# Edge gates of a graph-network kernel: one float32 product from the loaded features in place of three products from a rounded lead and rest

## What is computed

```
x_norm = layernorm(h);  q, k, v = x_norm @ Wq.T + bq, x_norm @ Wk.T + bk, x_norm @ Wv.T + bv
dk = silu(edge_attr @ Wdk.T + bdk)          # the "gates": 64 -> 256
dv = silu(edge_attr @ Wdv.T + bdv)          # 64 -> 256
attn = sum(q[dst] * k[src] * dk, axis=1)    # one number for an edge
attn = silu(attn) * cosine_cutoff(r)
msg  = v[src] * dv * attn[:, None]
agg  = segment_sum(msg, dst);  out = x + agg @ Wo.T + bo
```

## Time and profile before

| | |
|---|---|
| Median of 3 runs | 3666.56 us (3665.77 to 3671.32) |
| The profiled execution | 3659.42 us |
| Its span, first to last instruction | 3657.6 us |
| TensorE's granted clock, mean | 0.974 |
| TensorE busy | 3381.2 us, 92% of the span |
| VectorE busy | 3185.6 us, 87% |
| ScalarE busy | 2594.7 us, 71% |
| GpSimd busy | 2390.0 us, 65% |

### The profile page before, as it was taken

The page is one execution under the profiler, slowest core; times in us unless marked ns, Lnnn a source line. Parts: engine busy times, 40 slices in busy tenths (PEclk is TensorE's granted clock), DMA queues, the critical chain, the costliest instruction groups (busy, mean ns, idle before and its releaser), DMA issues. The chain is left out here.

```text
span 3657.6 us, 111781 instructions
## 1 busy us (share of the span) xinstructions
PE 3381.2 (92%) x25829; PEld 2771.8 (76%) x25830; DVE 3185.6 (87%) x9898; ACT 2594.7 (71%) x7607; POOL 2390.0 (65%) x2549
## 2 busy tenths in 40 slices
PE   3979999999999997996999999999999999997997
PEld 2547777777777775775888888888888888886996
DVE  6768999999999995664999999999999999996775
ACT  1856777777777774543878888888888888884553
POOL 3756777777777763554666666666666666663775
PEclk8989999999999997998999999999999999998998
DMA  3979999999999984776888888888888888884663
GB/s 102 263 230 309 301 296 301 298 298 298 299 298 300 300 253 165 276 258 224 254 235 239 240 236 239 237 239 237 238 238 239 238 237 239 236 237 150 213 208 126
DMA packets 604966, 898.40 MB, mean 246 GB/s; under 512 B 208971, under 2 KB 418646, under 8 KB 604371
## 3 DMA queue, kind: packets, MB, share of 16 engines
q0 software_dynamic: 164240, 566.71, 50.5%
q1 hardware_dynamic: 440643, 330.78, 30.2%
HBM read 724.25 MB, written 175.28 MB: 246 GB/s over the span
## 5 line engine op out<-in xcount | busy, mean ns | idle before, releaser
L1595 POOL DMA_INDIRECT kv1c<-kv_table,rec x900 | 865.9, 962 | 299.0 <-issue 284.6
L916 POOL DMA_INDIRECT kv<-kv_table,rec x832 | 848.3, 1020 | 282.3 <-issue 258.2
L1700 DVE CUSTOM_DVE_ANT_0 masked_scores<-score_p,far 126x384 f32<-126x384 f32 x1200 | 595.6, 551 | 30.2 <-issue 14.1
L1640 ACT ACTIVATE wv<-kv1c,wv 128x64 f32<-128x64 f32 x2400 | 605.9, 335 | 17.7
L954 ACT ACTIVATE gates<-gates_p 128x512 f32<-128x512 f32 x832 | 448.3, 591 | 77.5 <-PE gates_p L1087 77.5
L1803 PE MATMUL sum_p<-wv,hot 128*126 128x260 f32 x1800 | 477.7, 402 | 1.4 <-ACT wv L1640 1.4
L1759 PE MATMUL qe_p<-qrel,hotT 126*128 126x256 f32 x1800 | 443.0, 382 | 22.7 <-ACT hotT L1625 18.1
L1107 PE MATMUL sum_p<-msg,hot_weighted 128*124 128x256 f32 x1664 | 416.2, 393 | 5.3 <-ACT hot_weighted L962 5.3
L1759 PEld LDWEIGHTS qe_p<-qrel,hotT 126*128 126x128 f32 x1800 | 343.7, 191 | 74.9 <-ACT hotT L1625 18.7
L1107 PEld LDWEIGHTS sum_p<-msg,hot_weighted 128*124 128x124 f32 x1664 | 295.2, 187 | 116.2 <-issue 73.9
L1803 PEld LDWEIGHTS sum_p<-wv,hot 128*126 128x126 f32 x1800 | 316.1, 189 | 76.1 <-ACT wv L1640 1.8
(11 more groups left out here) (285 smaller groups left out, 7392.0 us busy)
## 6 DMA issues: line engine op xcount, KB each, us to landing
key<-segment_keys SPq DMA_DIRECT2D x300, 192.0 KB
q_blk<-q_table SPq DMA_DIRECT2D x208, 256.5 KB
acc_table<-acc SPq DMA_DIRECT2D x300, 130.0 KB
qrel<-q_by_relation SPq DMA_DIRECT2D x300, 128.0 KB
feat<-in_edge_feat_t SPq DMA_DIRECT2D x208, 128.0 KB
agg_and_x_plus_h<-total SPq DMA_DIRECT2D x208, 128.0 KB
kv1c<-kv_table,rec POOLq DMA_INDIRECT x900
kv<-kv_table,rec POOLq DMA_INDIRECT x832
```

The costliest lines, as they stand in the source:

```text
L916: pool.indirect_dma_start(kv[it.slot(AHEAD)][:, t, :], None, c["kv0_d"], bass.IndirectOffsetOnAxis(ap=rec[k][:, t, 0:1].bitcast(I32), axis ...
L1595: pool.indirect_dma_start(kv[k][:, t, :], None, c["kv1_d"], bass.IndirectOffsetOnAxis(ap=rec[k][:, t, 0:1].bitcast(I32), axis=0)).then_inc ...
L1640: ins = act.activation(wv[k][:, t, h, 0:DK], kv[s][:, t, D + h * DK:D + (h + 1) * DK], ACT.Copy, scale=wv[k][:, t, h, DK:DK + 1])
L1700: dve.tensor_tensor_reduce(junk[k][:, h], score_p[:, :, h, :], far[it.slot(U1)][:], 1.0, FLOOR, ALU.subtract, ALU.max, top[s][:, h:h + 1]) ...
```

## The change

The gates of a tile become the bias and one product in plain float32 of the loaded features `feat` and the loaded weights `w_raw`. `split_lead`, `split_rest`, their buffers, their semaphores and the split of the weights go. TensorE waits for the three loads of the chunk instead of `rest_ready`. The bias stays as it is, in float32r.

```diff
-                run_chunks(act, steps, ((1, hot_out), (0, split_lead), (2, attn_silu), (1, gates_silu(1)),
+                run_chunks(act, steps, ((1, hot_out), (2, attn_silu), (1, gates_silu(1)),
                                         (2, weigh_hot), (0, gates_silu(0))), U)
...
-                dve.tensor_copy(w_lead[:], w_raw[:])
-                dve.tensor_copy(b_rows[:], b_raw[:]).then_inc(w_lead_ready, 1)
-                dve.tensor_copy(b_lead[:], b_raw[:]).then_inc(w_lead_ready, 1)
-                dve.wait_ge(w_lead_ready, 2)
-                dve.tensor_tensor(w_rest[:], w_raw[:], w_lead[:], ALU.subtract).then_inc(w_ready, 1)
+                dve.tensor_copy(b_rows[:], b_raw[:]).then_inc(b_lead_ready, 1)
+                dve.tensor_copy(b_lead[:], b_raw[:]).then_inc(b_lead_ready, 1)
+                dve.wait_ge(b_lead_ready, 2)
...
                 run_chunks(dve, steps, ((2, q_times_k), (2, messages), (2, scores), (0, one_hot), (0, same_block),
-                                        (0, split_rest), (2, weights), (3, add_total)), U)
+                                        (2, weights), (3, add_total)), U)
...
-                    k = it.slot(2)
-                    wait(pe, rest_ready, it)
+                    s = it.slot(U)
+                    wait_slot(pe, loaded, it, LOADS)
                     for pair in range(PAIR):
...
                         for t, rows in tiles:
                             pe.matmul(gates_p[t][:], ones_r[rows, :], b_rows[rows, :], start=True, stop=False)
                         for t, rows in tiles:
-                            pe.matmul(gates_p[t][:], lead[k][rows, pair, :], w_lead[rows, :], start=False, stop=False)
-                        for t, rows in tiles:
-                            pe.matmul(gates_p[t][:], lead[k][rows, pair, :], w_rest[rows, :], start=False, stop=False)
-                        for t, rows in tiles:
-                            pe.matmul(gates_p[t][:], rest[k][rows, pair, :], w_lead[rows, :],
+                            pe.matmul(gates_p[t][:], feat[s][rows, pair, :], w_raw[rows, :],
                                       start=False, stop=True).then_inc(gates_summed, 1)
```

More of the change, by code:

```diff
@@ L794, in edges_0 @@
         w_raw, b_raw = sb("w_edge_raw", [P, 2 * D]), sb("b_edge_raw", [P, 2 * D])
-        w_lead, w_rest = sb("w_edge_lead", [P, 2 * D], F32R), sb("w_edge_rest", [P, 2 * D], F32R)
         b_lead, b_rows = sb("b_edge_lead", [P, 2 * D], F32R), sb("b_edge_rows", [P, 2 * D], F32R)
@@ L800, in edges_0 @@
         feat = [sb(f"feat{k}", [P, PAIR, P]) for k in range(U)]
-        lead = [sb(f"feat_lead{k}", [P, PAIR, P], F32R) for k in range(2)]
-        rest = [sb(f"feat_rest{k}", [P, PAIR, P], F32R) for k in range(2)]
         q_blk = [sb(f"q_blk{k}", [P, Q_ROW]) for k in range(U)]
@@ L821, in edges_0 @@
         w_loaded, filled = sem("w_edge_loaded"), sem("edge0_filled")
-        w_lead_ready, w_ready = sem("w_lead_ready"), sem("w_edge_ready")
-        lead_ready, rest_ready = sem("feat_lead_ready"), sem("feat_rest_ready")
+        b_lead_ready, w_ready = sem("b_edge_lead_ready"), sem("w_edge_ready")
         loaded, gathered = sems("edge0_loaded", U), sems("kv0_gathered", U)
@@ L925, in _ @@
                 steps = chunk_steps(act, c["steps0"])
[L927 to L931, removed]
                 def hot_out(it):
@@ L1011, in q_times_k @@
                     dve.tensor_tensor(qe_p[:], qe_p[:], kv[it.slot(AHEAD)][:, :, 0:D], ALU.mult).then_inc(qk_ready, 1)
[L1013 to L1017, removed]
                 def scores(it):
@@ L1056, in _ @@
                 run_chunks(dve, steps, ((2, q_times_k), (2, messages), (2, scores), (0, one_hot), (0, same_block),
-                                        (0, split_rest), (2, weights), (3, add_total)), U)
+                                        (2, weights), (3, add_total)), U)
             @block.tensor
             def _(pe):
-                pe.wait_ge(w_ready, 3)
+                pe.wait_ge(w_ready, 2)
                 steps = chunk_steps(pe, c["steps0"])
```

## The result

| | before | after |
|---|---|---|
| Median | 3666.76 us (3665.77 to 3671.32, 6 runs) | 3698.53 us (3689.81 to 3699.96, 6 runs) |
| Profiled execution | 3659.42 us | 3697.73 us |
| Span | 3657.6 us | 3695.9 us |
| Mean granted clock | 0.974 | 0.975 |

The ratio is 1.0076, 95% interval 1.0064 to 1.0087, and the medians stand 31.8 us apart. I had forecast 3711 us, 44 us more than before, and a range that begins at 3699 us. The direction and the mechanism held; the 44 us were more than a third too many, and the range began too high.

A forecast was written before the change was run, and what follows sets the result against it. VectorE was taken as the bound, TensorE 0.12 us behind; TensorE's round becomes 5.16 + 0.35 = 5.51 us against 5.29, +0.22 us over 200 chunks, +44 us: 3711 us on the median's scale, range 3699 to 3740 us.

The forecast's parts named there:

- VectorE sets the pace before, TensorE close behind: First edge stage: VectorE sets the chunk's 5.29 us, with TensorE only about 0.12 us behind.
- The loop through `qe_p` keeps the 0.34 us from being a gain: VectorE loses 0.34 us a chunk, but `q_times_k` still waits for `q_of_edges`; only about 0.02 us gained.
- TensorE's own round is 5.16 us: TensorE's chunk with nothing to wait for: about 5.28 - 0.12 = 5.16 us.
- A float32 pair's step is 0.434 us, the gates' +0.35 us: TensorE's gates: four float32 steps of 0.434 us added, 1.74 us, six old steps removed, 1.39 us.
- L1783's threes: Float32 products of 32 rows in three row groups, seen three at a time 0.11 us apart, taken as running side by side.
- Of 208 chunks 200 count: The +0.22 us applies to 200 of 208 chunks, since the first ones wait for gathers: +44 us.
- The sum on the scale of the median: Profiled 3659.4 + 44 = 3703 us; that execution is 7.1 us under the median, so 3666.6 + 44 = 3711 us.
- a little more slack: Range's lower end: with a float32 step of 0.427 us and slightly more TensorE slack, 3699 us.
- The serial pairs: Rival: float32 pairs don't run side by side; three steps +227 us, 3893 us, or four +407 us, 4073 us; 5 in 100.
- the slack isn't there: Rival: TensorE's loss ahead of `q_of_edges` is a fixed cost, so all added time counts: +73 us, 3740 us; 9 in 100.
- No slower: Rival: a 64-row float32 matmul costs no more than float32r, step under 0.38 us; 3662 us at best; 6 in 100.

The follow-up runs named there:

- before_swap: The kernel before with VectorE's `messages` step moved behind `scores`, nothing else; 3707.61 us against 3661.5 us, ratio 1.0134.
- no_rest: The kernel before without VectorE's rest instruction, the third gates product reading the lead instead; 3655.1 us against 3661.5 us, ratio 0.9985.
- after_no_bias_b: The changed kernel without the bias product of the gates; 3655.77 us against the kernel before at 3659.49 us, ratio 0.9986.
- no_rest_hot_b: The kernel before without the rest instruction, third product reading the lead, VectorE's order `q_times_k`, `one_hot`, `scores`, `messages`; 3629.33 us against 3659.49 us, ratio 0.9918.
- after_apart: The changed kernel with each tile's bias and float32 product together, run while transfers were late; 4484.7 us, ratio 0.990 to the kernel before.
- after_dead1: The changed kernel with a rest-sized VectorE instruction put back, result unread, run while transfers were late; 4486.17 us, ratio 0.9895 to the kernel before.
- after_no_bias: The changed kernel without the bias product of the gates, run while transfers were late; 4440.31 us, ratio 0.9814 to the kernel before.

## Why the prediction was wrong in size, point by point

- **VectorE sets the pace before, TensorE close behind.** That VectorE had nothing to spare is shown by `before_swap`: 0.27 us more for VectorE came out as 0.27 us more in the round. But the loop held the round just as tightly, so VectorE was not the bound alone.
- **The loop through `qe_p` keeps the 0.34 us from being a gain.** Shown twice: `no_rest` (0.9985) and `after_no_bias_b` (0.9986). That it is the loop is shown by `no_rest_hot_b`, which shortens it and gets 5.13 us.
- **TensorE's own round is 5.16 us. This step failed.** I read the time that TensorE loses, 0.12 us, from one chunk, and took it from a mean of 5.28. That chunk was right in itself: its 2.90 us from sum to turn became 2.78 us after. But it was one of the shorter rounds (5.26 us from sum to sum); the mean over the stage is 5.30 us and the bare round is 5.13 us (`no_rest_hot_b`). Over the 189 chunks of the kernel before that start from 330 to 1330 us, the stretch from sum to turn has a mean of 2.94 us, and in `no_rest_hot_b` 2.78: 0.16 us lost and not 0.12. TensorE's slack was 0.17 us a chunk by the rounds, so more of the products' cost was free: 0.03 us in the bare round and 0.01 us in the mean that it is set against, some 8 us in 200 chunks.
- **A float32 pair's step is 0.434 us, the gates' +0.35 us.** The step is 0.43 us and the gates' growth 0.33 to 0.34 us: another 2 to 3 us too many. That the pairs run side by side, read from L1783's threes in the earlier trace rows, is shown by the profile after. The Trainium skill (FP8 and Floating Point Precision, section TensorE Precision Notes) puts true float32 at four passes through the array. An estimate from that, 512 columns four times at 2.4 GHz, is 0.853 us; the two halves of a product take 2 x 0.43 = 0.86 us here, so the trace agrees.
- **Of 208 chunks 200 count.** Right: 34.2 us / 0.17 us = 201.
- **The sum on the scale of the median.** With 34 us in place of 44 it is 3666.6 + 34 = 3701 us, inside the range; the measured median is 2 us under this. The 7.1 us by which the profiled execution lay under its median didn't come again after the change (0.8 us), so the profiled executions stand 38.3 us apart and the medians 31.8.
- **The range.** The measured median lies 0.5 us under its lower end. That end allowed for a cheaper step and "a little more slack", not for the error of a slack read in a single chunk. 0.05 us either way on that reading, 10 us in all, would have been fair.
- **The rivals.** The serial pairs did not come: the halves stand 0.43 us apart, two at a time. That the slack isn't there is refuted: 0.17 of the 0.34 us were hidden. "No slower" was wrong in its premise (a step under 0.38 us).

## What to carry to other kernels

Where two engines are full and a third thing, a buffer with one copy, ties them, work out each one's own round and the loop's; an edit is worth only what it does to the largest of them. Here VectorE's row and the loop both stood at about 5.28 (the round they made was 5.30), TensorE at 5.13 and the gathers at 5.01 us, so taking 0.34 us off VectorE bought next to nothing and adding 0.34 us to TensorE cost half of that. Read the slack of the second engine as a mean over the stage, not from a chunk: when the forecast is a difference of two near numbers, a small error there weighs much. Here it was some 8 of the 12 us by which the forecast was too high. When reordering an in-order engine, look for an instruction that comes to stand straight behind the one it waits for.

## What the hardware showed that I had not expected

- A VectorE instruction that waits for the one directly ahead of it starts 0.27 us later than one that doesn't (1.41 us for 1.14 us behind a 128x1024 product, with the step's own semaphore instruction in it). One instruction of other work between them hides it: in `no_rest_hot_b` L1011, L995 and L1026 start at 804.27, 805.41 and 806.05 us, 1.14 and 0.64 us apart, as without a wait.
- Float32 products in two row groups (partitions 0 to 63 and 64 to 127) run side by side whatever the order in the source: 2.38 us of gates with the tiles taken apart, 2.37 us with them next to each other.
- A record's start alone misleads at a change of group. With nothing to wait for, the first matmul of `q_of_edges` is recorded 1.64 us after the first of `sum_messages` (the kernel after), and 1.88 us when it has to wait (the kernel before). But the group itself then shows 1.02 us for 1.14, so that the difference in that chunk is 0.12 us and not 0.24.
- Where the transfers came late, the changed kernel's variants were not slower than the kernel before: `after_apart` 0.990 (0.987 to 0.993), `after_dead1` 0.9895, `after_no_bias` 0.9814. Why is open; no run was made for it.
